# A new order for the end of the second stage, and its table stored by SyncE

## The reference, cut to what matters

```python
def _dcnv2(x, w_off, b_off, w, b, k, pad):
    om = conv(x, w_off) + b_off                    # offsets and mask
    oy, ox, mask = om[:, :P], om[:, P:2*P], sigmoid(om[:, 2*P:])
    val = _bilinear(x, oy + base_y, ox + base_x) * mask
    return einsum('ncphw,ocp->nohw', val, w) + b
# x: (8, 512, 52, 52) float32, 256 channels in the middle
h = _bn_lrelu(_dcnv2(x, w_off1, b_off1, w1, b1, 1, 0), g1, bb1, m1, v1)   # 1 tap
h = _bn_lrelu(_dcnv2(h, w_off2, b_off2, w2, b2, 3, 1), g2, bb2, m2, v2)   # 9 taps
return x + h
```

## Time and profile before

| | us |
|---|---|
| median of three runs | 3241.77 |
| lowest and highest | 3228.51, 3260.52 |
| profiled execution, device time | 3246.28 |
| its span, first to last instruction | 3244.3 |

### The profile page before, as it was taken

One profiled execution on the slowest core, in us unless ns is written; L12 is line 12 of the kernel. 1 busy time (PEld: TensorE's weight loads), 2 busy tenths in 40 slices (PEclk: granted clock), 3 DMA queues, 4 the chain that ended last, 5 costly groups with the idle time before them and its releaser, 6 DMA issues.

```text
span 3244.3 us, 48817 instructions
## 1 busy us (share of the span) xinstructions
PE 3042.3 (94%) x15660; PEld 2474.0 (76%) x15660; DVE 2741.7 (85%) x4746; ACT 2498.5 (77%) x4658; POOL 1744.9 (54%) x1708
## 2 busy tenths in 40 slices
PE   8997888889999999999999999999999999999999
PEld 7996455478777778777878777778777777777879
DVE  5557999879888889888989888889888888888987
ACT  5665777778787878788888787878788778778876
POOL 0003444456666566665666666666665656665652
PEclk9998999989999999999999999999999999999999
DMA  9998999999999999998999999999999999998995
GB/s 324 366 353 318 387 347 332 321 377 355 356 361 345 364 356 347 351 369 323 372 367 353 354 370 339 370 353 343 358 357 333 360 343 330 345 360 324 356 346 188
DMA packets 431464, 1125.10 MB, mean 347 GB/s; under 512 B 42956, under 2 KB 171468, under 8 KB 431232
## 3 DMA queue, kind: packets, MB, share of 16 engines
q0 software_dynamic: 244784, 891.09, 74.2%
q1 hardware_dynamic: 118608, 163.05, 14.1%
q10 hardware_dynamic: 67840, 68.16, 6.1%
HBM read 1002.15 MB, written 137.04 MB: 351 GB/s over the span
## 4 chain that ended last, share of the span: by engine, by line
PE 44%; DVE 32%; ACT 12%; issue 8%; another core or an unknown queue 3%; ACTq 1%; DMA 0%; SPq 0%; DVEq 0%; POOLq 0%
PE psum_t L1327 29%; DVE arena L1246 11%; DVE val_lo L1261 6%; PE psum_t L400 5%; PE psum_t L1314 5%; ACT psum_t L1195 5%; PE psum_t L730 4%; DVE arena L1254 4%; ACT arena L1203 2%; DVE val_first L1254 2%; DVE z_sb L1268 2%; ACT val_hi L1209 2%; DVE arena L877 2%; DVE arena L1278 1%
## 5 line engine op out<-in xcount | busy, mean ns | idle before, releaser
L1181 POOL DMA_INDIRECT arena<-table,plan_in x1521 | 1571.4, 1033 | 1017.6 <-DVE arena L1254 444.4
L1327 PE MATMUL psum_t<-val_hi,w_hi 128*128 128x512 f32 (+2 forms) x3096 | 1247.2, 403 | 50.9 <-ACT z_sb L1218 30.8
L1327 PE MATMUL psum_t<-val_hi,w_lo 128*128 128x512 f32 (+2 forms) x3096 | 1205.7, 389 | 8.9 <-issue 8.7
L1327 PE MATMUL psum_t<-val_lo,w_hi 128*128 128x512 f32 (+2 forms) x3096 | 1204.0, 389 | 4.5 <-issue 4.3
L1195 ACT ACTIVATE psum_t<-arena,plan_in 128x512 f32<-128x512 f32 x1521 | 1042.4, 685 | 211.6 <-DVE arena L1246 119.9
L1246 DVE SCALAR_TENSOR_TENSOR arena<-arena,plan_in,psum_t 128x512 f32<-128x512 f32 x1521 | 1129.3, 742 | 72.4 <-issue 38.6
L1327 PEld LDWEIGHTS psum_t<-val_hi,w_hi 128*128 128x128 f32 x3096 | 587.7, 190 | 187.8 <-ACT z_sb L1218 50.4
L1261 DVE TENSOR_TENSOR val_lo<-psum_t,val_hi 128x1024 fp32r<-128x1024 f32 (+2 forms) x387 | 465.5, 1203 | 275.3 <-ACT val_hi L1209 167.5
L1327 PEld LDWEIGHTS psum_t<-val_hi,w_lo 128*128 128x128 f32 x3096 | 586.0, 189 | 132.8 <-issue 11.8
L1327 PEld LDWEIGHTS psum_t<-val_lo,w_hi 128*128 128x128 f32 x3096 | 588.9, 190 | 108.1 <-issue 5.9
L1209 ACT ACTIVATE val_hi<-psum_t 128x1024 fp32r<-128x1024 f32 (+2 forms) x387 | 386.4, 998 | 272.7 <-remote 185.5
(11 more groups left out here) (90 smaller groups left out, 2396.8 us busy)
## 6 DMA issues: line engine op xcount, KB each, us to landing
arena<-x SPq DMA_DIRECT2D x90, 512.0 KB, 4.7
table<-arena ACTq DMA_DIRECT2D x40, 896.0 KB, 7.3
out<-arena SPq DMA_DIRECT2D x136, 256.0 KB
table<-arena ACTq DMA_DIRECT2D x40, 768.0 KB, 7.1
arena<-x SPq DMA_DIRECT2D x70, 384.0 KB, 6.3
arena<-table,plan_in POOLq DMA_INDIRECT x1521
table<-table SPq DMA_DIRECT2D x32, 512.0 KB
arena<-w POOLq DMA_DIRECT2D x9, 512.0 KB, 6.5
```

The costliest lines, as they stand in the source:

```text
L1181: nc.gpsimd.indirect_dma_start(landing(r, i)[:, :], None, rows, bass.IndirectOffsetOnAxis(ap=row.bitcast(u32), axis=0))\
L1327: last = nc.tensor.matmul(psum_acc[:, oc, 0:n], a[:, w, oc * P:(oc + 1) * P], b[:, r % 2, kt, 0:n], start=(w == 0 and a is w2_hi and b is ...
```

## The change

1. All stores of stage 2 to `table2` go from ACT's list to SP's. The last chunk's second store is cut in two, tiles 6 to 9 and 10 to 12 (`parts_of`, `LATE_TILE`).
2. PE's order in all of stage 2: a band is convolved from one step behind the pair that completes it (two calls in one step, the third in the next), where it was three, four and five steps behind its last tile. `turn` comes at 8 steps, not 9, the folds at 6, not 7, `keep_tail` at step 8 of a chunk, not 9.
3. ACT's drain is written out: units 0 to 5 come ahead of the folds of the last two bands and `upper` between these, then units 6 and 7. DVE follows; its `modulate` of the chunk before the last is put behind unit 3's `add_line`.
4. PE multiplies tap 0 ahead of `transpose(0, 1)`, in the order of banks 3, 1, 2, 0; only bank 0 waits for the offsets to be read.
5. Of the last plan only the first operation of `place` stays in the drain. The other five come at tap 7 of stage 3, `hats` at tap 8, `modulate` at tap 9. SP stores that plan later, and its work of stage 3 follows that store.
6. Slots: behind the three in odd h comes the one wholly in the transposed h, then the two in the folded offsets, and then the four that touch the even chunks' h.

```diff
+                def store_h(c):
+                    for half in range(2):
+                        for j, tiles in parts_of(c, half):
+                            sp.wait_ge(h_ready, c * CHUNK + j + tiles)
+                            table_writes(sp, table2, h_buf(c), c, (j, tiles), table2_written[c % 2][half], copies_of(c))
...
+                for c in range(CHUNKS):
+                    store_h(c)
+                    if c:
+                        store_plan(c - 1)
...
+                    for band, nth in CONVOLVE_AT.get(t, ()):
+                        convolve(band, nth)
+                    if t == TILES + 2:
                         begin_transpose()
-                    for nth in range(3):
-                        if t - 3 - nth in BAND_AT:
-                            convolve(BAND_AT[t - 3 - nth], nth)
...
+                    act.wait_ge(lines_ready, TILES - 1)
+                    begin_unit(0)
+                    fold_band(before_last, 1)
+                    copy_h_t(last_pair - 1)
+                    fold_band(before_last, 2)
+                    act.wait_ge(lines_ready, TILES)
+                    act.wait_ge(upper_added, TILES)
+                    begin_unit(1)
+                    copy_h_t(last_pair)
+                    for u in range(2, 6):
+                        begin_unit(u)
+                    for dy in range(3):
+                        fold_band(last_but_one, dy)
                     begin_upper()
+                    for dy in range(3):
+                        fold_band(last, dy)
+                    for u in range(6, BEGUN):
+                        begin_unit(u)
                     modulation(CHUNKS - 1)
-                    hats(CHUNKS - 1)
+                    return lambda: hats(CHUNKS - 1)
...
-                def begin_units():
-                    for u in range(BEGUN):
+                def begin_units(plan_ahead, offsets_read):
+                    for u in range(6):
                         add_far(0, u // GROUP_TILES, u % GROUP_TILES)
-                        if u >= 3:
-                            add_line(0, (u - 3) // GROUP_TILES, (u - 3) % GROUP_TILES)
+                        if u >= 2:
+                            add_line(0, 0, u - 2)
+                    plan_ahead()
                     lower(0, 0)
+                    add_far(0, 1, 2)
+                    add_line(0, 1, 0)
+                    add_far(0, 1, 3)
+                    offsets_read()
...
+                def begin_multiply(offsets_read):
+                    multiply(0, 0, order=(3, 1, 2, 0), first_free=offsets_read)
+                    transpose(0, 1)
```

More of the change, by code:

```diff
@@ L49 @@
 PLAN_AT = 6
+LATE_TILE = 10
+PLACE_REST_AT = 7
 PIECE = 2
@@ L287, in copies_of, with parts_of, written_to @@
             return 2 if c < WHOLE_CHUNKS else 1
-        def written_to(b, chunks):
-            return sum(copies_of(c) * 16 for c in range(b, chunks, 2))
+        def parts_of(c, half):
+            j, n = HALVES[half]
+            if c == CHUNKS - 1 and half == 1:
+                return (j, LATE_TILE - j), (LATE_TILE, j + n - LATE_TILE)
+            return ((j, n),)
+        def written_to(b, half, chunks):
+            return sum(copies_of(c) * len(parts_of(c, half)) * 16 for c in range(b, chunks, 2))
         def load_plan(sp, s):
@@ L295, in load_plan, with table_writes @@
             sp.dma_start(plan_in[:, s % 2, 0:n, :], plan2[:, t + 1:t + 1 + n, :]).then_inc(plan_loaded[s % 2], 16)
-        def table_writes(eng, table, source, c, half, written, copies=2):
-            j, n = HALVES[half]
+        def table_writes(eng, table, source, c, tiles, written, copies=2):
+            j, n = tiles
             for row, col in ((WIDTH, 0), (0, C_MID))[:copies]:
@@ L644, in second_stage, with complete_at @@
             BAND_AT = {last_tile(band): band for band in range(BAND_COUNT)}
+            def complete_at(band):
+                return next(t for t in range(last_tile(band), TILES) if t in PAIR_AT)
+            CONVOLVE_AT = {}
+            for band in range(BAND_COUNT):
+                for nth, after in enumerate((1, 1, 2)):
+                    CONVOLVE_AT.setdefault(complete_at(band) + after, []).append((band, nth))
             def band_pieces(band, dy):
@@ L837, in run @@
                     act.wait_ge(const_ready, 1)
-                    for t in range(TILES + DRAIN):
+                    for t in range(TILES):
                         if NEAR_AHEAD <= t + 1 < TILES:
@@ L1177, in step @@
                             pool.wait_ge(turned, BAND_COUNT)
+                        elif PLACE[u] == IN_H_STAGE[0]:
+                            for half in range(2):
+                                pool.wait_ge(table2_written[0][half], written_to(0, half, CHUNKS))
+                            pool.wait_ge(h_transposed, TILES)
                         rows = table2[0:image_end(r // TAPS) + WIDTH, :]
@@ L1239, in step, with go_on @@
                             evacuate(it, ended, EVACUATE[r % TAPS][i])
-                return begin_unit, lambda: upper(0, 0), lambda: in_full(step, after=5, first=2)
+                def go_on(late_hats):
+                    in_full(lambda it, r: step(it, r, late_hats), after=5, first=2)
+                return begin_unit, lambda: upper(0, 0), go_on
             def on_vector(dve):
@@ L1303, in step, with go_on @@
                                 op(it, ended, table[r % TAPS][i])
-                return begin_units, lambda: in_full(step, after=5, first=2)
+                def go_on(late_place, late_modulate):
+                    in_full(lambda it, r: step(it, r, late_place, late_modulate), after=5, first=2)
+                return begin_units, go_on
             def on_tensor(pe):
@@ L1316, in transpose, with multiply @@
                     last.then_inc(transposed, 1)
-                def multiply(it, r):
+                def multiply(it, r, order=range(KT1), first_free=None):
                     n, k = tiles_of(r) * P, r % TAPS
                     pe.wait_ge(lo_ready, taps_to(it, r))
-                    for oc in range(KT1):
+                    for oc in order:
+                        if oc == 0 and first_free:
+                            first_free()
                         if k == 0 and exists(it, r - 1):
```

106 lines of the change are left out of this document (52 added, 54 removed).

## The result

The changed kernel takes 3257.69 us (median of 20 runs, 3253.17 to 3269.99), the kernel before 3244.61 in the runs beside it (20 runs, 3228.51 to 3260.52): a ratio of 1.0045 with an interval from 1.0034 to 1.0056. It is 13 us slower, within 1% as forecast. The forecast of 3229, though, was for a gain, and the measurement lies above its range of 3212 to 3250. In all that follows, ratios leave out the few executions that stand far outside the others of the same kernel (3221.71 us beside 3073, 13172.95 beside 3253); medians are of all executions.

A forecast was written before the change was run, and what follows sets the result against it. DVE was taken to set the pace in stage 2 and PE in stage 3. Terms -10.9 (drain), -4.0 (stores) and +2.4 (PE's order) made -12.5 us, giving 3229 us on the median; range 3212 to 3250.

The forecast's parts named there:

- PE's order in stage 2: Stage 2: pairs transposed about 1.1 us late, PE catching up; +0.2 us a chunk, +2.4 in all, bounds -4.7 and +13.
- The rival that named it: Stage 2: PE's order costs DVE 1.45 to 2.9 us a chunk, at 2.9 3262 us in all; chance 0.10.
- my sign for it: Stage 2 in the new profile: DVE below 24 busy of every 25.5 us would show that PE's order costs DVE.
- Stores by SP: Stage 2: with stores issued by SP, nobody waits behind the issue that had held ACT; -4.0 us, bounds 0 and -6.
- The first units ahead of the folds: Drain after stage 2: ACT's early units let tap 0's transposes start at about 633.5 us, not 641.25.
- Tap 0 multiplied at once: Drain into stage 3: tap 0's multiply starts at 638.5 us; tap 1's first matmul at 650.4 against 661.34, 10.9 us earlier.
- PE's wait of 4 us: Drain: PE stands from 644.9 to 649.5 us for DVE before tap 2's transposes, already counted in the sum.
- The stall waits for the drain: Tap 1: the 11.0 us stall ends near 666 us, 6 us before 672.22; gain 10, 3232 us; within the forecast's 0.55.
- Gathers and slots: Seam of stages 2 and 3: gathers of units 11 and 12 come early enough to cost nothing; 0, bounds 0 and +3 us.
- The late plan: Stage 3, taps 7 to 9: about 2 us of moved small operations fit in 2.4 us; 0, bounds 0 and +4 us.
- no dent in PE at taps 7 to 9: Stage 3 in the new profile: a sign that the operations moved to these taps do not hold PE.
- The head start goes through to the end: Stage 3: from 677.81 us to the end takes 2566 us as before, so every microsecond gained earlier comes off the end.

The follow-up runs named there:

- e2_sp_stores: The kernel before with all stores to the second table issued by SP, the last plan where it was: 3250.37 us, ratio 1.0001.
- e4: The kernel before with gathers held to 12 units ahead from unit 18 on, instead of 18 ahead; slow chip: 3243.24 us, ratio 0.9978.
- e6: The changed kernel with PE's old order in chunks 0 to 11 and gathers held to 12 ahead; quick chip: 3072.66 us, 0.999 against the kernel before.
- d1: The kernel of e6 measured once more on the quick chip, against the kernel before: 3072.26 us, ratio 0.9993.
- e7: The changed kernel, all parts, with gathers held to 12 units ahead; quick chip: 3081.11 us, 1.0018 against the kernel before.
- e8: The changed kernel with PE's old order in chunks 0 to 11, gathers held to 10 ahead only for units 18 to 59: 3073.2 us, 0.9993 against the kernel before.
- f1: The kernel of e8 with the last plan finished in the drain as before, not at taps 7 to 9: 3070.47 us, 0.9985 against the kernel before.

## Why the prediction was right or wrong, step by step

- **What failed.** Between the forecast's -12.5 us and the +13 measured lie two steps. PE's order in stage 2 was priced at a fifth of what it cost, and the head start of the drain was let through to the end, where on this chip it was gone by tap 11. Either alone would have left the time in the range.
- **PE's order in stage 2 (+2.4): the step that turned a gain into a loss.** The direction and the mechanism were there, a pair 1.1 us late, ACT's copy with it. I then took 0.2 a chunk because PE's total has slack and "it catches up", and left 1.1 a chunk for the bound (+13). The chunk's measured price is 1.1, and in all stage 2 ends 12.5 us later in one pair of profiles, 14 in the mean of the slow chips' four old and three new ones. I had priced the late pair but not PE's own new waits for ACT (29.6 us in ten chunks), with which it doesn't catch up. The rival that named it put break-even at 1.24 a chunk; at a price of 1.1 it would still have given a gain of 1.7, since it took the other terms as they stood. And my sign for it, DVE under 24 busy of 25.5 us, was set too low: DVE is busy 24.43.
- **Stores by SP (-4.0): the stall right, the gain mostly not.** The stall of 4.42 us went as foreseen; the next two chunks repaid over half in e2_sp_stores and nearly all in the mean of all profiles, and its runs show nothing at the end (1.0001). The Trainium skill, page "DMA: Bandwidth & Descriptors", section "Issuing engines are not separate DMA queues", came nearer with its rule that another issuer saves little, for another reason: the sequencer's time here was not little (5.91 us), it was just not what set the end.
- **The first units ahead of the folds (part 3): right.** Tap 0's transposes were foreseen 7.9 us behind the last `activate` and stand 8.0, in the changed kernel's both profiles; tap 1's foreseen 18.4, measured 19.8.
- **Tap 0 multiplied at once (part 4, -10.9 with part 3): nearly right in size, not in worth.** Without stalls tap 1's first matmul comes 9.2 us sooner and tap 2 10.0, tap 3 only 7.3, since PE's wait of 4 us, which I had named, brings matmuls at the lower clock, which I had not. On the slow chip 2.4 to 4.8 us are left at tap 5.
- **The stall waits for the drain (named in the 0.55): half right.** Its length did depend on the gathers, as e4 shows, but there isn't one shorter stall. ACT has two or three, 16 to 17 us together, in all four slow-chip profiles of the new drain. That the stall might be split, I had not considered. The -10 I wrote for this rival doesn't follow from its terms either: a stall that ends 6.2 us sooner, -4.0 and +2.4 make -7.8.
- **Gathers and slots (0): right.** Unit 11's gather was foreseen 7.6 us behind the last `activate`, unit 12's 12.9; in the timeline of POOL they stand 8.1 and 13.6 behind (PE's `convolve` and `turn` release them):

```profile
646.25 0.94 POOL L1224 DMA_INDIRECT arena<-table,plan_in  x1 [2.64 <-PE psum_t L759]
...
651.70 0.94 POOL L1224 DMA_INDIRECT arena<-table,plan_in  x1 [4.51 <-PE psum_t L777]
```

- **The late plan (0, bound +4): inside the bound, its own cost not shown.** Taps 10 to 20 take 1.0 to 2.9 us more with it (e6, d1, e7, e8) and 1.4 more without (f1). What it surely moves is SP's work, where I had looked only at when the residual is wanted: in the kernel after the first load stands behind the plan's store and comes at 718.04 instead of 678.03, in one burst with the others. I had expected no dent in PE at taps 7 to 9; on the quick chip there is none (d1, e6), on the slow one tap 9 is long in all four profiles of the new drain (8.6 to 9.4), with the wait for remote ahead of it, as told above. SP's queue in the kernel after:

```profile
646.37 66.69 SPq L700 DMA_DIRECT2D plan<-plan_sb  x2
718.04 0.90 SPq L1132 DMA_DIRECT2D arena<-x  x2
...
727.30 5.70 SPq L303 DMA_DIRECT2D plan_in<-plan  x1
```

- **The head start goes through to the end: the second step that failed.** I had said that from tap 3's transposes on 2566 us are left. It is 2583.4 in the first profile after and 2554.6 in the second: stalls of the steady part move it by more than the whole change, and the end can't be judged from single profiles of the slow chip. The first taps can. Behind the last `activate`, tap 11's transposes stand 101.9 to 104.5 us in the four slow profiles of the new drain and 99.3 to 104.2 in the four of the old one with the same 18 ahead: each new one has had one more wait for remote there, of 5 to 6 us, and nothing is left of the head start. Why that wait comes is not shown. On the quick chip, with 12 ahead, 7.3 us are left at tap 11, and stage 3 is 3.6 longer to the end.
- **The sum as it came out:** stage 2 +12.5 and from there to tap 11 +0.4 in the first pair of profiles, in all +12.9, against 13.1 and 13.0 between the medians of the two sets of runs (15.9 by the second set's ratio). The rest of stage 3 is 10.4 us longer in that pair and shorter in the other; the medians say that it evens out.

The prediction had one idea of what the stall is: a fetch of instructions held up behind the gathers. The Trainium skill, page "Runtime: NRT & Kernel Launch", section "Instruction fetch mechanics", says that instructions come by DMA in blocks and that this is mostly hidden; that gathers could hold a fetch up is not on the page but was mine. The trace shows such packets on queues of their own (110 of them with 1.80 MB on queue 8). That the stall shortens with the row of gathers would agree. Against it speaks the trace: no instruction packet lies in the stalls of the seam, and the next one starts after them. No other cause was tested.

## What to carry to other kernels

A consumer moved next to its producer can cost the round trip between engines, even when each engine's total still fits. So count the work between two due times and follow the circle of waits, before taking an engine's slack as cover. When an order must be changed for the end of a loop, change it there only; here the switch then costs 3 us in the last chunk, not 9 to 14 over all. And a head start, or a stall that is removed, is worth what is left of it some steps further on: follow it tap by tap against a common mark, here the last `activate`, before it is counted at the end.

## What the runs showed of the hardware that I had not expected

- The same kernel takes 3075 us on some chips and 3240 to 3248 on others. On the former PE is busy in all of 800 us of stage 3, on the latter in 768, with 16 waits of ACT put down to remote, up to 6.5 us long, and 24 of DVE without a name, up to 3.5; the quick chips' profiles have none of either.
- The old drain's wait of this kind took 8.9 to 13.3 us in four profiles with gathers 18 units ahead and 5.1 to 5.2 in two with 12.
- In it PE stood up to 2.4 us between two matmuls of one tap, with no wait in the program, and no instruction packet was moved from 650 to 675 us.
- Four microseconds in which PE stood were followed by a stretch of 4 us with the granted clock at 0.53, and a tap of 9.17 instead of 6.33 us.
- Gathers 8 units ahead instead of 18 cost 15.8%; 12 ahead, with the new drain, cost 1.6 to 3.4 us of 2294 on the quick chip.
